# Expert weights summed once and loaded by DMA, and the two routed groups of a layer run side by side

## The reference

```python
h = relu(flat @ Wi.T + bi)                                  # 256 wide
for l in range(2):
    shared = (einsum('nd,shd->snh', h, Ws[l]) + bs[l]).mean(axis=0)     # one shared expert
    routed = sum over e of where(route == e, h @ Wr[l, e].T + br[l, e], 0)
    h = relu(shared + routed + h)
out = h @ Wo.T + bo
```

## Time and profile before

| | |
|---|---|
| median of 3 runs | 1025.38 us |
| span of the profiled execution, first to last instruction | 1013.7 us |
| median less span | 11.7 us |
| PE busy | 993.1 us (98%) |
| PEld, DVE, ACT, POOL busy | 529.6, 416.6, 310.8, 179.0 us |
| DMA | 220.57 MB, mean 218 GB/s |

### The profile page before, as it was taken

One profiled execution on the slowest core, in us unless ns is written; L12 is line 12 of the kernel. 1 busy time (PEld: TensorE's weight loads), 2 busy tenths in 40 slices (PEclk: granted clock), 3 DMA queues, 4 the chain that ended last, 5 costly groups with the idle time before them and its releaser, 6 DMA issues.

```text
span 1013.7 us, 12482 instructions
## 1 busy us (share of the span) xinstructions
PE 993.1 (98%) x3618; PEld 529.6 (52%) x3618; DVE 416.6 (41%) x1443; ACT 310.8 (31%) x601; POOL 179.0 (18%) x216
## 2 busy tenths in 40 slices
PE   8999999999999999999997999989999999999997
PEld 4555555555555444444443588734545445454554
DVE  6323223323313344334434156562453424535266
ACT  4644645645541000000001254241312223122231
POOL 4110010010010122121222144551011010110101
PEclk9999999999999999999999899989999999999999
DMA  9995675366104788888854743167464564645300
GB/s 363 421 416 196 258 319 241 133 290 277 56 0 167 296 331 301 309 306 305 323 207 170 266 120 112 31 215 280 166 258 178 188 239 166 257 179 187 156 1 22
DMA packets 41664, 220.57 MB, mean 218 GB/s; under 512 B 6644, under 2 KB 22712, under 8 KB 29430
## 3 DMA queue, kind: packets, MB, share of 16 engines
q1 hardware_dynamic: 38454, 215.21, 55.2%
q0 software_dynamic: 2864, 4.39, 1.3%
q10 hardware_dynamic: 272, 0.13, 0.0%
HBM read 210.29 MB, written 11.62 MB: 219 GB/s over the span
## 4 chain that ended last, share of the span: by engine, by line
PE 93%; ACT 3%; DVE 1%; issue 1%; DMA 1%; DVEq 0%; POOL 0%; SPq 0%; ACTq 0%; POOLq 0%
PE PA L1822 22%; PE PA L1573 22%; PE PA L1593 22%; PE O L1768 3%; PE O L1886 3%; ACT U L682 3%; PE O L1642 3%; PE PA L1551 2%; PE T L1906 2%; PE T L1895 1%; PE SR L1886 1%; PE SM L1886 1%; PE O L1614 1%; PE O L1604 1%; PE O L1863 1%
## 5 line engine op out<-in xcount | busy, mean ns | idle before, releaser
L1822 PE MATMUL PA<-ring,S 128*128 128x512 f32 x512 | 236.0, 602 | 3.4 <-issue 3.4
L1593 PE MATMUL PA<-ring,S 128*128 128x512 f32 x512 | 229.8, 595 | 1.2 <-DMA ring<-in_adj_cols 1.2
L1573 PE MATMUL PA<-ring,U 128*128 128x512 f32 x512 | 226.7, 595 | 0.0
L1573 PEld LDWEIGHTS PA<-ring,U 128*128 128x128 f32 x512 | 94.8, 190 | 106.6 <-issue 106.5
L1593 PEld LDWEIGHTS PA<-ring,S 128*128 128x128 f32 x512 | 95.4, 190 | 102.4 <-issue 98.7
L1822 PEld LDWEIGHTS PA<-ring,S 128*128 128x128 f32 x512 | 92.9, 192 | 103.8 <-issue 100.5
L602 ACT ACTIVATE work<-ring 128x2048 int8<-128x2048 f32 x64 | 122.2, 1910 | 9.0 <-issue 4.7
L1429 DVE TENSOR_TENSOR U<-ring,work 128x512 f32<-128x512 f32 x112 | 81.8, 735 | 89.4 <-PE SR L1886 45.5
L750 ACT ACTIVATE work<-T,work 128x64 f32<-128x64 f32 x112 | 29.0, 310 | 66.8 <-PE T L1895 54.2
L847 POOL DMA_INDIRECT disp_d<-work x32 | 31.9, 997 | 96.4 <-DVE work L1263 89.1
L859 POOL DMA_INDIRECT y_d<-R,work x40 | 39.3, 983 | 51.1 <-DVE R L1331 41.1
(11 more groups left out here) (271 smaller groups left out, 1086.4 us busy)
## 6 DMA issues: line engine op xcount, KB each, us to landing
ring<-in_adj_cols SPq DMA_DIRECT2D x52, 2048.0 KB, 9.3
ring<-in_adjT_cols SPq DMA_DIRECT2D x32, 2048.0 KB, 7.2
ring<-in_adj_cols SPq DMA_DIRECT2D x8, 1024.0 KB, 13.6
work<-in_w SPq DMA_DIRECT2D x16, 256.0 KB, 2.8
ring<-in_Wr SPq DMA_DIRECT2D x1, 4096.0 KB, 12.1
ring<-in_Wr SPq DMA_DIRECT2D x2, 2048.0 KB, 13.3
disp_d<-U SPq DMA_DIRECT2D x4, 650.0 KB, 19.4
work<-disp_d SPq DMA_DIRECT2D x8, 325.0 KB, 3.7
```

Source lines behind the costliest of these rows:

```text
L1573: mm = nc.tensor.matmul(out_T[:, :], X[:, t * D:(t + 1) * D], ring[slot][t // HT][:, (t % HT) * BW:(t % HT + 1) * BW], start=n == 0, stop= ...
L1593: mm = nc.tensor.matmul(PA[k % 2][:, :], S[:, t * D:(t + 1) * D], ring[slot][t // HT][:, (t % HT) * BW:(t % HT + 1) * BW], start=t == 0, s ...
L1822: mm = nc.tensor.matmul(PA[slot][:, :], S[:, t * D:(t + 1) * D], ring[1][t // HT][:, (t % HT) * BW:(t % HT + 1) * BW], start=t == 0, stop= ...
```

## The change

- The sums `Wr + Ws + I` of all 32 matrices are made once, in the expert stage: DVE adds `w_s` to eight slices of four experts each (`add_self`), four before expert 0 and one behind each of experts 0 to 3. SP stores each slice (1 MB) to a DRAM tensor `w_d` (`STORED` tells behind which expert's weights).
- In stage 3 DVE's `stage_w` is gone. SP reads the route of each segment into a register and loads the 256 KB of its summed weight from `w_d` into one of 16 buffers in `ring[0]` (`load_group`), a group of four as soon as PE is done with that group of the block before. The refills of `ring[1]` stand in the same queue, in the order shown.
- `TAIL3` runs both groups of a layer in one piece, and some pieces move by a tile or two.
- `Wr` is loaded by quarters during the last step of stage 2, no longer at its end and in the expert stage; `WsT` is loaded and gets its diagonal in stage 2. `w_s` shares its SBUF with weights of stage 1. The last block uses the same 16 buffers as the others.

```diff
+        w_d = nc.dram_tensor("w_d", [L2 * E2, P, KH * DH], F32).ap()
-        WS = 4
-        wst = [U[:, KH * BW + KH * DH * i:KH * BW + KH * DH * (i + 1)] for i in range(WS)]
+        wst = [ring[0][1][:, KH * DH * i:KH * DH * (i + 1)] for i in range(L2 * SB)]
+        SLICE = 4
+        NS = L2 * E2 // SLICE
+        STORED = ((), (), (0,), (1,), (2, 3), (4,), (5, 6), (7,))
...
 # SP, tail_inputs (stage 2)
+                sp.dma_start(w_s, A["WsT"]).then_inc(s_wself, 16)
 # SP, ahead of the expert stage
-            sp.wait_ge(s_agg2, NB)
-            sp.wait_ge(s_sc, 16 * (NT - BT))
-            sp.dma_start(ring[0][0][:, :], A["Wr"][0]).then_inc(s_ring[0][0], 16)
-            sp.dma_start(ring[0][1][:, 0:QUART], A["Wr"][1, :, 0:QUART]).then_inc(s_ring[0][2], 16)
+            for n, q in enumerate(ORDER2):
+                if n < 3:
+                    sp.wait_ge(s_quart2, (NB - 1) * 3 + n + 1)
+                else:
+                    sp.wait_ge(s_agg2, NB)
+                at = q % 2 * QUART
+                sp.dma_start(ring[0][q // 2][:, at:at + QUART], A["Wr"][q // 2, :, at:at + QUART]).then_inc(s_ring[0][q], 16)
...
 # SP, expert loop, behind load_weights(e, e % 2)
+                for i in STORED[e]:
+                    sp.wait_ge(s_pre, i + 1)
+                    alone(sp)
+                    sp.dma_start(w_d[SLICE * i:SLICE * (i + 1)].rearrange("e p n -> p e n"), slice_of(i)).then_inc(s_wkept, 16)
...
 # SP, stage 3, behind the loads of y
+            def load_group(k, g):
+
+                if k > 1:
+                    sp.wait_ge(s_wu, (k - 2) * (L2 * SB) + (g + 1) * SH)
                     alone(sp)
+                for n in range(g * SH, (g + 1) * SH):
+                    l, s = n // SB, n % SB
+                    e = sp.value_load(route_sb[0:1, ds((k - 1) * SB + s, 1)], min_val=0, max_val=E2 - 1)
+                    sp.dma_start(wst[n], w_d[ds(e + l * E2, 1)].rearrange("o p n -> (o p) n")).then_inc(s_wg[g], 16)
...
+            sp.wait_ge(s_wkept, 16 * NS)
+            for g in range(NG):
+                load_group(1, g)
+            for q in range(4):
+                refill3(1, q)
+            for b in range(2, NB + 1):
+                if b < NB:
+                    refill3(b, 0)
+                load_group(b, 0)
+                if b < NB:
+                    refill3(b, 1)
+                load_group(b, 1)
+                load_group(b, 2)
+                if b < NB:
+                    refill3(b, 2)
+                load_group(b, 3)
+                if b < NB:
+                    refill3(b, 3)
...
 # DVE, expert stage
+            def add_self(i):
+
+                l = i // (NS // L2)
+                if i % 2 == 0:
+                    dve.wait_ge(s_ring[0][i // 2], 16 * 8)
+                    alone(dve)
+                shared = w_s[:, l * KH * DH:(l + 1) * KH * DH].unsqueeze(1).to_broadcast([P, SLICE, KH * DH])
+                nc.vector.tensor_tensor(slice_of(i), slice_of(i), shared, ALU.add).then_inc(s_pre, 1)
+
             for e in range(2):
                 tags(e, e)
+            for i in range(4):
+                add_self(i)
             for e in range(E1):
                 expert(e, e % 2, e // 2 if e >= 2 else None)
                 if e + 2 < E1:
                     tags(e + 2, e % 2)
+                if e + 4 < NS:
+                    add_self(e + 4)
...
 # DVE, inner_step3
-                for n in range(2, L2 * SB):
-                    stage_w(k, n)
-                    if n in RAW_AT:
-                        raw_rows(k, RAW_AT.index(n))
-                raw_rows(k, NG - 1)
...
+                for g in range(NG):
+                    raw_rows(k, g)
...
 # PE, routed
-                weights = wst if k < NB else last_w
+                pe.wait_ge(s_wg[g], 16 * SH * k)
...
 # PE
-            TAIL3 = [(2, turn_sum), (10, turn_hn3), (12, h0), (14, lambda k: routed(k, 0)), (17, lambda k: routed(k, 1)),
-                     (17, lambda k: turn_routed(k, 0)), (18, lambda k: turn_routed(k, 1)), (21, lambda k: routed(k, 2)),
-                     (24, lambda k: routed(k, 3)), (24, lambda k: turn_routed(k, 2)), (25, lambda k: turn_routed(k, 3)),
-                     (31, out_proj), (NT, None)]
+            def layer(k, l):
+                routed(k, 2 * l)
+                routed(k, 2 * l + 1)
+
+            TAIL3 = [(2, turn_sum), (9, turn_hn3), (11, h0), (14, lambda k: layer(k, 0)), (16, lambda k: turn_routed(k, 0)),
+                     (17, lambda k: turn_routed(k, 1)), (22, lambda k: layer(k, 1)), (24, lambda k: turn_routed(k, 2)),
+                     (25, lambda k: turn_routed(k, 3)), (31, out_proj), (NT, None)]
```

More of the change, by code:

```diff
@@ L64 @@
 NG = L2 * SB // SH
-RAW_AT = (5, 8, 15)
 ORDER1 = (7, 6, 5, 4, 3, 2, 0, 1)
@@ L221, in build @@
         b_last = small[:, 48:48 + L2 * KH * SB].rearrange("p (lm s) -> p lm s", lm=L2 * KH, s=SB)
-        last_w = [ring[1][0][:, KH * DH * i:KH * DH * (i + 1)] for i in range(L2 * SB)]
-        raw = [U[:, KH * BW + KH * DH * WS + BW * i:KH * BW + KH * DH * WS + BW * (i + 1)] for i in range(2)]
+        raw = [U[:, KH * BW + BW * i:KH * BW + BW * (i + 1)] for i in range(2)]
         mv3 = e_rows[0][:, 0:2 * NT]
@@ L372, in build @@
         s_h0 = sem("s_h0")
-        s_wst = sem("s_wst")
+        s_wself = sem("s_wself")
+        s_pre = sem("s_pre")
+        s_wkept = sem("s_wkept")
+        s_wg = [sem(f"s_wg{g}") for g in range(NG)]
         s_wu = sem("s_wu")
@@ L568, in _, with refill3 @@
                 sp.dma_start(tiles(R[:, lo * D:hi * D], hi - lo), y_t[:, lo:hi, :]).then_inc(s_yin[c], 16)
[L571 to L576, removed]
-                    alone(sp)
-                    load_quarter(sp, adjT, b, 1, q)
+            def load_group(k, g):
+                if k > 1:
+                    sp.wait_ge(s_wu, (k - 2) * (L2 * SB) + (g + 1) * SH)
+                    alone(sp)
+                for n in range(g * SH, (g + 1) * SH):
+                    l, s = n // SB, n % SB
+                    e = sp.value_load(route_sb[0:1, ds((k - 1) * SB + s, 1)], min_val=0, max_val=E2 - 1)
+                    sp.dma_start(wst[n], w_d[ds(e + l * E2, 1)].rearrange("o p n -> (o p) n")).then_inc(s_wg[g], 16)
+            def refill3(b, q):
+                if q < 3:
+                    sp.wait_ge(s_quart3, (b - 1) * 3 + q + 1)
+                else:
+                    sp.wait_ge(s_agg3, b)
+                alone(sp)
+                load_quarter(sp, adjT, b, 1, q)
+            sp.wait_ge(s_wts3, 16 * len(F2_INPUTS))
+            sp.wait_ge(s_wkept, 16 * NS)
[16 more added lines that the diff above has]
+                    refill3(b, 3)
             sp.wait_ge(s_out, NB + 1)
@@ L1283, in step2, with self_weights @@
                 route(k)
+            def self_weights():
+                dve.wait_ge(s_wself, 16)
+                alone(dve)
+                for l in range(L2):
+                    for kk in range(KH):
+                        diag = w_s[:, (l * KH + kk) * DH + kk * P:(l * KH + kk) * DH + (kk + 1) * P]
+                        nc.vector.tensor_tensor(diag, diag, ident[:, :], ALU.add)
             for k in range(1, NB - 1):
                 step2(k, k % 2, (k + 1) // 2)
+                if k == 3:
+                    self_weights()
             for k in (NB - 1, NB):
@@ L1414, in _ @@
                         last.then_inc(s_hid, 1)
[L1417 to L1430, removed]
             def raw_rows(k, g):
-                dve.wait_ge(s_wu, (k - 1) * (L2 * SB) + (g + 1) * SH + WS)
+                dve.wait_ge(s_wu, (k - 1) * (L2 * SB) + (g + 1) * SH)
                 alone(dve)
@@ L1887, in routed @@
                                                   src[:, kk * BW + s * SEG:kk * BW + (s + 1) * SEG],
[L1888 removed]
+                                                  wst[n0 + c][:, kk * DH:(kk + 1) * DH], start=kk == 0, stop=kk == KH - 1)
                             if kk == KH - 1:
```

39 lines of the change are left out of this document (14 added, 25 removed).

## The result

| | time, us (median of timed runs) | ratio to before, 95% interval |
|---|---|---|
| before | 1025.28 (1025.15 to 1025.98) | |
| forecast | 1020.1, range 1018.3 to 1025.0 | |
| after | 1016.67 (1014.73 to 1017.69) | 0.9913 (0.9899 to 0.9927) |

The profiled execution of after took 1014.73 us, with a span of 1013.0. So 1.7 us lie outside the span. That number is the first thing that doesn't fit: for before the prediction had put 11.7 us outside it.

A forecast was written before the change was run, and what follows sets the result against it. TensorE (PE), busy 93% of the span, was taken as the bound. Routed groups run together in seven steps gave -5.3 us and everything else 0, so 1025.38 became 1020.1 us, range 1018.3 to 1025.0.

The forecast's parts named there:

- the same against the median of the three runs: Whole kernel: the 5.3 us saved in the 1013.7 us span also comes off the 1025.38 us median.
- Summing in the expert stage: Expert stage: DVE's eight adds of 2.29 us fit its waiting gaps; cost 0, upper bound about 4 us.
- Side by side: Last stage's steps: a layer's routed groups run together, 0.77 us less per step, seven steps 5.4, taken as 5.3.
- Rival 1: Last stage's steps: price is per group, not per change; only 2.7 us gained, 1022.7 us; chance 0.15.
- rival 4: Last stage's steps: the switch costs more than seen; 6.6 us gained, 1018.8 us; chance 0.06.
- upper end: Routed groups in the steps: half of all 1.48 us overhead and the transposes' 0.20 go, 0.94 x 7 = 6.6 us.
- Staged adds out: Last stage: 112 adds of 0.735 us and the last block's 16 leave DVE; PE never waits for them, worth nothing.
- SP's price: SP's queue, last stage: 0.8 us for each register load and dynamic load, bounds nothing and 1.7 us.
- rival 3: SP's queue: SP becomes the bound from 1.7 us per load, 1033.8 us at 2.5; chance 0.07 including a DVE overrun.
- The moved pieces and the stores: Last stage's moved tail pieces are fed in time; expert stage's eight 1 MB stores leave rows 1.9 us in hand, cost 0.
- Rival 2: Expert stage: rows of experts 5 and 7 late behind stores; at 150 GB/s costs 13.4 us, 1033.5 us; chance 0.10.
- The last block: End of last stage: raw copy comes earlier, but PE's own second group ends later than that copy; nothing gained.

The follow-up runs named there:

- The repeated execution: The kernel before, unchanged, profiled again: 1024.82 us (ratio 0.9996); its profiled execution took 1023.92 us with a span of 1021.8.
- experiment 4: The kernel after with DVE's eight adds in the expert stage cut from 128x2048 to 128x16 columns: 1019.46 us (ratio 0.9945).

## Why the prediction was wrong, step by step

- **The step that failed** is the last of the sum: the same against the median of the three runs, "which lies 11.7 us above the span for what is outside it". About 2 us lie outside the span. Most of the rest were standstills in the expert stage and behind it. The repeated execution, whose time is near that of the timed runs, is 8.1 us longer: 6.1 in the expert stage and 2.7 in the reading back, less 0.6 of an earlier start. The one the prediction read had none. With them taken for a constant, nothing that the change does to the expert stage could show in the sum.
- **"Summing in the expert stage: cost 0"** is the term that should have held them. Its bounds were 0 and +4 us, no gain thought of. Measured by experiment 4 it is some -3 (uncertain by 2.5): the adds pull GpSimd's scatters apart and so shorten the standstills. With the 4.96 of the last stage that makes 8 of the 8.6 us; the remaining 0.6 is within what single executions differ by. Which engine shares what with GpSimd was not asked, though GpSimd's rows stand beside the gaps that the adds were to fill.
- **Side by side** was sized well: 0.77 us a step forecast, 0.61 measured, 0.71 with the 0.10 that the rest of the change gives. The 3.60 us of the last block held to the digit. Rival 1 (per group, 0.39 a step) is out, as the second group of a layer takes 1.82 us in the step above (755.56 to 757.38) and not 1.88, and so is rival 4. Its upper end of 6.6 us was a wrong sum besides: the transposes' 0.20 is part of the 1.48, so half of the other 1.28 and the 0.20 make 0.84 a step, 5.9 us.
- **Staged adds out: nothing.** The rest of the change gives 0.10 us a step, 0.7 us in all, in rows of PE that wait for nothing. That it is the staged adds that slowed them was not tried by itself.
- **SP's price** was too low: 0.8 us was taken for a register load and a load, and sixteen took 18.90 us, 1.18 each (timeline of SP's queue in after):

```profile
661.50 4.70 SPq L584 DMA_DIRECT2D R<-y_d  x8
667.29 18.90 SPq L595 DMA_DIRECT2D ring<-w_d  x16
686.33 11.82 SPq L399 DMA_DIRECT2D ring<-in_adjT_cols  x4
```

  The first refill went out at 686.33 and not at 674.4: 6.1 us of that are the price, the rest is that SP was free of the loads of y later (first load at 667.29, not 661.6). It landed 7.7 us after its issue, at 694.0, and PE comes to it near 697.6, so 3.5 us are left of the 13 that the prediction had to spare, and PE waits for no ring (rival 3 would have begun at 1.7 us each).
- **The moved pieces and the stores** went as said: the rows of experts 5 and 7 came in time, DVE took up expert 0 at 579.99, and the output projection stands 12 products and 0.2 us behind the transposes as before. Rival 2 did not occur.
- **The last block**: nothing forecast, nothing measured, as seven steps of 0.71 are all that the last stage lost.

The forecast of what the change does itself, 5.3 us, was meant for the last stage and is to be read against its 4.96. That it also agrees with the 5.6 of the kernels without scatters rests on the 0.57 at the start, which may be chance. Some 3 us of the rest come from a disturbance of the kernel before that the profile at hand did not show.

Open is why a row of five scatters holds up PE's signals in most executions and did not in the first: its rows of scatters were five in a row as well. Where in the chip the signals wait was not tried. The first execution differs in one more row of the page, the scatters' median time to landing, which no later page has a value for. First execution of before, then the repeated one:

```profile
y_d<-R,work POOLq DMA_INDIRECT x40, 2.3
```

```profile
y_d<-R,work POOLq DMA_INDIRECT x40
```

So the landing signals too were recorded otherwise. That the disturbance lies in how these signals are passed on is a guess, not shown.

## What to carry to other kernels

Put the profiled execution's span beside the timed runs first; if they are further apart than what lies outside a span (2 us here), the trace lacks something that the clock sees, and the sum has to say what. An engine that stands with all its inputs ready is read together with what the other queues do at that moment: two engines that start within 0.01 us of each other, as here at 604.28 and at 644.01, were probably held by one thing. Long rows of GpSimd scatters beside a tight hand-over between engines deserve a gap; here 1.3 us after the third scatter was worth 4 to 5 us in before, and nothing measurable in after, whose adds already part most rows.

## What was not expected of the hardware

- While GpSimd issued five indirect DMAs in a row, other engines took up PE's finished work up to 2.7 us later than usual in before (a lag of 3.53 against 0.8), mostly 1.0 to 1.4 us behind the row's last instruction, and 4.6 us later once in after beside a row of eight (5.33 against 0.7). With a gap of 1.3 us in each row of before they did not, and in one execution of before they did not without a gap either.
- One add of 128x2048 on DVE lengthened a scatter of 0.97 us to 2.4 to 2.6 us; two adds of 128x896 only to 1.2.
- The level of a kernel moved by 4 us between comparisons, with before at 1024.9 to 1025.3 in three and at 1021.4 in two others, and after with it (1016.7, 1016.4 and 1011.9), while the ratio stayed at 0.991. So only kernels of one comparison are set against each other to a few us.
